# A transformer layer with dense experts on eight cores: layernorm's square root, squares and applies moved from ScalarE to VectorE, and one rope moved to GpSimd

## The chip, the cores and the metric

The kernel runs on all 8 cores of one Trainium2 chip. Each core takes one of the 8 batch rows (4096 tokens of 1024 channels) and runs the same program; the cores do not talk to each other. The metric is the device time of the slowest core in microseconds. The weights are loaded by every core from f32 in HBM and kept in bf16.

## What is computed

Per batch row, with `ln` a layernorm over the 1024 channels (eps 1e-5):

```python
h = ln(x)
q, k, v = h @ Wq, h @ Wk, h @ Wv               # 16 heads of 64
q, k = rope(silu(q)), rope(silu(k))
energy = einsum('bnhd,bmhd->bhnm', q, k) * tril
o = einsum('bhnm,bmhd->bnhd', energy, v)
o = o * sigmoid(h @ Wg1 @ Wg2)
x = x + ln((ln(o) * gamma + beta) @ Wo)
t = ln(x)
w = softmax over the top 2 of 8 of silu(t @ rw1 + rb1) @ rw2 + rb2
y = t + sum_e w_e * (silu(t @ ew1[e] + eb1[e]) @ ew2[e] + eb2[e])
x = x + ln(y)
```

The energy has no softmax, so the kernel computes attention chunk by chunk with a running state of k times v. There are five layernorms for every token.

## The kernel before

The program has three stages, each a block of its own. An `emit` records an instruction for one engine, with the tokens (semaphore and count) that it waits for; the five queues run in the order of recording. VectorE, ScalarE and GpSimd instructions always wait for the instruction before them on their own engine, through the engine's own semaphore, in addition to what `after` names.

**Attention (stage A)** works through 32 chunks of 128 tokens. For each i it records the front of chunk i and then the back of chunk i-1.

- `emit_front`: the tables cos and sin come by DMA (SP's queue, after both ropes of the chunk before). `emit_ln_stats` makes rstd and -mean*rstd of x (VectorE sum, ScalarE Square with accumulator, four small VectorE steps L298 to L307, Sqrt on ScalarE L310, reciprocal and two products on VectorE L313 to L318). ScalarE applies them (L378), PE transposes, ScalarE copies, PE does the q, k and v projections (L399, L410, L429), ScalarE applies Silu to q and k (L417, L421) and Tanh to the gate (L459). VectorE copies v (L463) and does q's rope (six instructions, L333 to L343), GpSimd does k's rope with the same helper, VectorE finishes the gate (L475). PE transposes q and k (L481, L490). Then 16 heads follow one another: energy on PE (L506), mask on VectorE (L513), three matmuls on PE. At the end VectorE updates the state (L537, L542) and makes `og`, output times gate (L545).
- `emit_back`: layernorm of `og` (apply L565), transposes (L573), the product with Wo (L583) into the PSUM tile pbig0, its layernorm (apply L600), the sum x1 with the residual (L604) and its store and the load of a later x on SP, layernorm of x1 (apply L619), a store of t, transposes (L629) and a copy into `tT`, which stays in SBUF for all 4096 tokens.

The four layernorms of a chunk use one scratch tile of columns for the front and one for the back. On VectorE the back of chunk i-1 is recorded behind the whole front of chunk i, so its first step runs after L545 of chunk i.

**Router (stage B)** computes the expert weights; the diff does not touch it.

**Experts (stage C)** goes over two groups of 2048 tokens. Each group first puts the weighted bias into `yac` for 16 chunks (PE L873, ScalarE copy L889), then all 8 experts run for all tokens (PE L909 and L946, Silu on ScalarE L920, the weighted sum on VectorE L959). Then comes the tail: for each of 16 chunks SP loads x1 and t (L977, L980) once the store of the chunk before has landed, VectorE adds t (L983), `emit_ln3` makes the statistics (Square L828 on ScalarE, sum L831 and small steps L833 to L842 on VectorE, Sqrt L845, then L848 to L853), ScalarE applies (L994), VectorE adds x1 (L997), SP stores.

Of the kernel before, what the change touches and what calls it, by code (L numbers as in the profile page):

```python
# [127 lines left out]
def build(debug=False, n_chunks=NCH, phases="ABC", stage=999):  # L128
# [32 lines left out]
    with ExitStack() as octx:  # L161
# [9 lines left out]
        with ExitStack() as actx:  # L171
# [118 lines left out]
            def emit_ln_stats(colbuf, src_ap, after_tok, psum_src=False):  # L290
                c_sx, c_sq, c_m, c_a, c_msq, c_b, c_s, c_rs, c_mrs, c_nmrs = range(10)
# [6 lines left out]
                t_m = s.emit(V, lambda e: e.tensor_scalar(  # L298
                    colbuf[:, c_m:c_m + 1], colbuf[:, c_sx:c_sx + 1], 1.0 / E, None,
                    ALU.mult), after=[t_sx])  # L300
                t_a = s.emit(V, lambda e: e.tensor_scalar(
                    colbuf[:, c_a:c_a + 1], colbuf[:, c_sq:c_sq + 1], 1.0 / E, EPS,
                    ALU.mult, ALU.add), after=[t_sq])
# [751 lines left out]
```

How the kernel before makes its waits and increments, by code:

```python
            def body(eng):  # L90
                waited = {}
                for waits, fn, semname, inc in recs[ename]:
                    for s, v in waits:
                        if waited.get(s, 0) >= v:
                            continue
                        eng.wait_ge(sems[s], v)
                        waited[s] = v
                    inst = fn(eng)
                    inst.then_inc(sems[semname], inc)
                for s, v in extra_final:
                    if waited.get(s, 0) >= v:
                        continue
                    eng.wait_ge(sems[s], v)
                    waited[s] = v
```

## Time and profile before

| | us |
|---|---|
| median of 6 runs | 7287.3 (7280.26 to 8089.09) |
| profiled execution, its own time | 7279.65 |
| its span, slowest core | 7277.9 |
| spans of the eight cores | 7258.9 to 7277.9 |
| busy in that span: PE, DVE, ACT, POOL | 4893.5, 1390.4, 1572.2, 299.0 |

PE is TensorE, DVE VectorE, ACT ScalarE, POOL GpSimd, SP the sync engine whose queue issues most DMAs. The times include a few microseconds around the span. Busy shares are averages over stages with different limits, so the stages are read one by one: attention lasts until 2828 us, the router until 3121 us, the experts of the first group until 4966.7 us, its tail until 5198.6 us; the second group's tail begins after 7042 us.

### The profile page before, as it was taken

How to read it: one execution, taken by the hardware profiler on the slowest of the kernel's cores; microseconds unless marked ns; L12 is line 12 of the kernel's file. 1: busy time of each engine (PE TensorE's matmuls, PEld its weight loads, DVE VectorE, ACT ScalarE, POOL GpSimd, SP SyncE). 2: the span in 40 equal slices, each digit the busy share in tenths (PEclk: the TensorE clock that was granted, in tenths of full speed). 3: DMA queues.
4: the chain of work that ended last, by engine and by line, in shares of the span. 5: the costliest groups of instructions: out<-in, count | busy, mean ns of one | idle time of the engine just before them, and what ended most of it. 6: DMA issues, size and time to landing. Idle time of an engine off the chain costs nothing.

```text
span 7277.9 us, 62772 instructions; the slowest of 8 cores (7258.9 to 7277.9 us)
## 1 busy us (share of the span) xinstructions
PE 4893.5 (67%) x22618; PEld 2257.1 (31%) x23024; DVE 1390.4 (19%) x2892; ACT 1572.2 (22%) x2185; POOL 299.0 (4%) x236
## 2 busy tenths in 40 slices
PE   3444344444444445479999999992399999999960
PEld 1222222222222222224444444441144444444430
DVE  1232322322323221210000000002100000000013
ACT  1222222222222222222211121111212211122111
POOL 1000001100000000000000000000000000000000
PEclk7666666666666666689999999996699999999985
DMA  3000000000000001022202222011111222112202
GB/s 60 21 21 21 27 25 21 21 21 21 21 21 25 26 21 21 1 51 47 47 10 38 47 47 47 16 31 58 58 24 24 47 47 47 25 23 47 47 22 90
DMA packets 92129, 241.52 MB, mean 33 GB/s; under 512 B 7528, under 2 KB 7784, under 8 KB 91824
## 3 DMA queue, kind: packets, MB, share of 16 engines
q0 software_dynamic: 54096, 136.65, 10.8%
q1 hardware_dynamic: 37728, 100.83, 4.1%
q8 instruction: 189, 3.10, 0.2%
q14 instruction: 116, 0.95, 0.0%
HBM read 332.15 MB, written 41.94 MB: 51 GB/s over the span
## 4 chain that ended last, share of the span: by engine, by line
PE 49%; DMA 3%; DVE 2%; ACT 2%; issue 1%; SPq 0%; DVEq 0%; ACTq 0%; POOLq 0%
PE peo L946 24%; PE peh L909 24%; DMA tc<-ts 2%; DMA out<-x1c 1%; ACT ehb L920 1%; ACT ylnb L994 1%; DVE yf L983 1%; DVE sc L831 1%; DVE x1c L997 1%; PE peo L873 0%; ACT yac L889 0%; SPq L977 0%; DVEq L96 0%; ACT sc L845 0%; DVE sc L848 0%
## 5 line engine op out<-in xcount | busy, mean ns | idle before, releaser
L946 PE MATMUL peo<-ew_bf,ehb 128*128 128x512 bf16 x8028 | 1769.4, 379 | 76.7 <-ACT ehb L920 68.2
L909 PE MATMUL peh<-tT,ew_bf 128*128 128x512 bf16 x8028 | 1772.4, 379 | 9.4 <-issue 0.7
L920 ACT ACTIVATE ehb<-peh,eb_sb 128x512 bf16<-128x512 f32 x1024 | 704.2, 688 | 2851.8 <-PE peh L909 2851.7
L946 PEld LDWEIGHTS peo<-ew_bf,ehb 128*128 128x128 bf16 x8192 | 797.1, 98 | 1049.0 <-issue 97.5
L909 PEld LDWEIGHTS peh<-tT,ew_bf 128*128 128x128 bf16 x8192 | 802.0, 98 | 970.9 <-issue 6.8
L959 DVE SCALAR_TENSOR_TENSOR yac<-peo,wsb,yac 128x1024 bf16<-128x1024 f32 x256 | 328.7, 1284 | 3368.6 <-PE peo L946 3356.6
L518 PE MATMUL pbig<-vb,eT 128*128 128x64 bf16 x512 | 108.8, 213 | 279.1 <-DVE eT L513 279.1
L629 PE MATMUL ptr<-identbf,sb_o 128*128 128x128 bf16 x256 | 32.4, 306 | 391.2 <-ACT sb_o L619 391.2
L513 DVE TENSOR_TENSOR eT<-pm,trium 128x128 bf16<-128x128 f32 x512 | 149.4, 292 | 638.6 <-PE pm L506 638.6
L573 PE MATMUL ptr<-identbf,sb_o 128*128 128x128 bf16 x256 | 32.4, 306 | 286.4 <-ACT sb_o L565 286.4
L873 PE MATMUL peo<-eb_bf,wTsb 8*128 8x512 bf16 x64 | 31.8, 595 | 277.1 <-ACT yac L889 269.8
L310 ACT ACT_TABLE_LOAD x32 | 41.1, 1283 | 812.6 <-DVE scol L307 812.6
L399 PE MATMUL pbig<-Wq_bf,ln1T 128*128 128x512 bf16 x511 | 171.5, 509 | 40.3 <-ACT ln1T L390 40.3
L583 PE MATMUL pbig<-Wo_bf,qT 128*128 128x512 bf16 x480 | 161.9, 496 | 51.7 <-ACT qT L576 51.7
L481 PE MATMUL ptr<-identbf,qro 128*128 128x128 bf16 x256 | 32.4, 306 | 239.2 <-DVE qro L343 239.2
L506 PE MATMUL pm<-qT,kTt 64*128 64x128 bf16 x512 | 144.7, 283 | 39.9 <-ACT kTt L493 39.9
L518 PEld LDWEIGHTS pbig<-vb,eT 128*128 128x128 bf16 x512 | 53.4, 104 | 359.7 <-issue 359.7
L385 PE MATMUL ptr<-identbf,ln1b 128*128 128x128 bf16 x256 | 32.4, 306 | 193.2 <-ACT ln1b L378 193.2
L629 PEld LDWEIGHTS ptr<-identbf,sb_o 128*128 128x128 bf16 x256 | 24.8, 138 | 399.8 <-issue 399.8
L808 POOL DMA_DIRECT2D ew_bf<-ew x15 | 13.2, 878 | 3278.7 <-PE peh L909 3278.7
L695 PE MATMUL pr<-tT,rw_bf 128*128 128x512 bf16 x498 | 132.1, 430 | 21.2 <-DMA rw_bf<-rw 19.4
L333 POOL TENSOR_TENSOR kt<-ks,sinb 128x512 f32<-128x512 f32 x32 | 40.4, 1262 | 2448.2 <-PE pbig L429 2357.8
(138 smaller groups left out, 3180.0 us busy)
## 6 DMA issues: line engine op xcount, KB each, us to landing
ew_bf<-ew POOLq DMA_DIRECT2D x30, 4096.0 KB, 26.3
xb<-x SPq DMA_DIRECT2D x32, 512.0 KB, 4.2
x1s<-x1b SPq DMA_DIRECT2D x32, 512.0 KB, 2.9
x1c<-x1s SPq DMA_DIRECT2D x32, 512.0 KB, 3.8
out<-x1c SPq DMA_DIRECT2D x32, 512.0 KB, 2.6
cosb<-cosr SPq DMA_DIRECT2D x32, 256.0 KB, 2.8
sinb<-sinr SPq DMA_DIRECT2D x32, 256.0 KB, 3.0
ts<-sb_o SPq DMA_DIRECT2D x32, 256.0 KB, 2.0
```

Source lines behind the costliest of these rows:

```text
L399: return e.matmul(pbig0[:, nh * 512:(nh + 1) * 512], ln1T[:, k, :], Wq_bf[:, k, nh * 512:(nh + 1) * 512], start=(k == 0), stop=(k == KT - 1))
L506: e.matmul(pe_slot[:, 128:256], kTt[po:po + 64, tile, :], qT[po:po + 64, tile, :], start=True, stop=True),
L513: e.tensor_tensor(eT[:, slot, :], pe_slot[:, 128:256], trium[:, :], ALU.mult),
L518: t_intra_last = s.emit(T, lambda e, h=h, slot=slot: e.matmul(pbig1[:, h * 64:(h + 1) * 64], eT[:, slot, :], vb[:, h * 64:(h + 1) * 64], s ...
L583: return e.matmul(pbig0[:, nh * 512:(nh + 1) * 512], qT[:, k, :], Wo_bf[:, k, nh * 512:(nh + 1) * 512], start=(k == 0), stop=False)
L695: return e.matmul(pr[:, :], rw1_bf[:, k, m * 128:(m + 1) * 128], tT[:, k, t8 * 512:(t8 + 1) * 512], start=(k == 0), stop=(k == KT - 1))
L831: t_sx = s3.emit(V, lambda e: e.reduce_sum(sc3[:, c_sx:c_sx + 1], src_ap, axis=AX.X), after=after_tok)
L909: return e.matmul(ph[:, :], ew1_bf[:, k, m * 128:(m + 1) * 128], tT[:, k, tstart:tstart + 512], start=(k == 0), stop=(k == KT - 1))
L920: e.activation(ehb[:, m, :], ph[:, :], AF.Silu, bias=eb1_sb[:, eidx, m:m + 1]),
L946: return e.matmul(po[:, nh * 512:(nh + 1) * 512], ehb[:, k, sub * 128:(sub + 1) * 128], ew2_bf[:, k, nh * 512:(nh + 1) * 512], start=(k == ...
L959: return e.scalar_tensor_tensor(yac[:, ci, :], po[:, :], wsb[:, ch0 + ci, eidx:eidx + 1], yac[:, ci, :], ALU.mult, ALU.add)
L983: t_y = s3.emit(V, lambda e, ci=ci: e.tensor_tensor(yf[:, :], yac[:, ci, :], tc[:, :], ALU.add), after=[t_tc, t_yacc_last[ci]] + ([t_prev_ ...
```

## The change

Three edits, in stage A and in the tail of stage C.

- Sqrt on ScalarE and reciprocal on VectorE are replaced by a reciprocal square root made of VectorE instructions on one column: a first guess from the bits of the number (five instructions) and three Newton steps of four instructions. This holds for all five layernorms.
- The apply moves from ScalarE (scale and bias) to VectorE (subtract the mean, multiply by rstd) for all layernorms but the front one, which keeps ScalarE and the two products (`emit_nmrs`). The squares of the og and x1 layernorms move to VectorE; those of x, of Wo's output and of the tail stay on ScalarE. In the tail the sum is now recorded before the Square.
- q's rope moves from VectorE to GpSimd, where it is recorded ahead of k's.

```diff
+            def emit_rsqrt(colbuf, c_v, c_out, after):
+                ci = colbuf[:, :].bitcast(I32)
+                t = s.emit(V, lambda e: e.tensor_scalar(
+                    ci[:, 20:21], ci[:, c_v:c_v + 1], 1, None,
+                    ALU.logical_shift_right), after=after)
+                s.emit(V, lambda e: e.tensor_copy(colbuf[:, 21:22], ci[:, 20:21]))
+                s.emit(V, lambda e: e.tensor_scalar(
+                    colbuf[:, 22:23], colbuf[:, 21:22], -1.0, MAGIC,
+                    ALU.mult, ALU.add))
+                s.emit(V, lambda e: e.tensor_copy(ci[:, 23:24], colbuf[:, 22:23]))
+                s.emit(V, lambda e: e.tensor_copy(
+                    colbuf[:, c_out:c_out + 1], ci[:, 23:24].bitcast(F32)[:, 0:1]))
+                for _ in range(3):
+                    s.emit(V, lambda e: e.tensor_tensor(
+                        colbuf[:, 20:21], colbuf[:, c_out:c_out + 1],
+                        colbuf[:, c_out:c_out + 1], ALU.mult))
+                    s.emit(V, lambda e: e.tensor_tensor(
+                        colbuf[:, 21:22], colbuf[:, c_v:c_v + 1],
+                        colbuf[:, 20:21], ALU.mult))
+                    s.emit(V, lambda e: e.tensor_scalar(
+                        colbuf[:, 22:23], colbuf[:, 21:22], -0.5, 1.5,
+                        ALU.mult, ALU.add))
+                    t = s.emit(V, lambda e: e.tensor_tensor(
+                        colbuf[:, c_out:c_out + 1], colbuf[:, c_out:c_out + 1],
+                        colbuf[:, 22:23], ALU.mult))
+                return t
...
-                t_sq = s.emit(S, lambda e: e.activation(
-                    dump[:, :], src_ap, AF.Square,
-                    accum_out=colbuf[:, c_sq:c_sq + 1]),
-                    after=after_tok + ([t_sx] if psum_src else []))
+                if sq_eng == "S":
+                    t_sq = s.emit(S, lambda e: e.activation(
+                        dump[:, :], src_ap, AF.Square,
+                        accum_out=colbuf[:, c_sq:c_sq + 1]),
+                        after=after_tok + ([t_sx] if psum_src else []))
+                else:
+                    t_sq = s.emit(V, lambda e: e.scalar_tensor_tensor(
+                        dump[:, :], src_ap, 1.0, src_ap, ALU.mult, ALU.mult,
+                        accum_out=colbuf[:, c_sq:c_sq + 1]), after=after_tok)
...
-                t_s = s.emit(S, lambda e: e.activation(
-                    colbuf[:, c_s:c_s + 1], colbuf[:, c_b:c_b + 1], AF.Sqrt),
-                    after=[t_b])
-                t_rs = s.emit(V, lambda e: e.reciprocal(
-                    colbuf[:, c_rs:c_rs + 1], colbuf[:, c_s:c_s + 1]), after=[t_s])
...
+                t_rs = emit_rsqrt(colbuf, c_b, c_rs, [t_b])
+                return ([t_rs], colbuf[:, c_rs:c_rs + 1],
+                        colbuf[:, c_m:c_m + 1])
...
+                ln_toks, rs_ap, nmrs_ap = emit_nmrs(scol, ln_toks)
...
-                t_ropeq = emit_rope(V, qs, rt2, qro,
+                t_ropeq = emit_rope(GP, qs, rt2, qro,
...
-                t_oln = s.emit(S, lambda e, rs_ap=rs_ap, nmrs_ap=nmrs_ap,
-                               ogs=ogs:
-                               e.activation(sb_o[:, :], ogs, AF.Identity,
-                                            bias=nmrs_ap, scale=rs_ap),
+                    sq_eng="V")
+                t_oln = s.emit(V, lambda e, rs_ap=rs_ap, m_ap=m_ap, ogs=ogs:
+                               e.tensor_scalar(sb_o[:, :], ogs, m_ap, rs_ap,
+                                               ALU.subtract, ALU.mult),
```

The applies `t_aoln`, `t_tb` and, in the tail, `t_yln` change in the same way as `t_oln`; the x1 layernorm has `sq_eng="V"` too; `emit_ln3` gets its own copy of the reciprocal square root.

## Rows read from the trace of the kernel before

In the view of stretches (rows 1) the columns are the stretch and its length, the busy us of each engine with its instructions in brackets, PEclk, the DMA share and GB/s. In a timeline (rows 2, 3, 4, 6) they are start and busy us, engine, line, operation, tiles, count, and in brackets the idle time before with what ended it. In the view of groups (rows 5) busy us and mean ns of one stand behind the first bar, idle us before them behind the second.

**Rows 1.** Busy time by stretch: attention, experts of group 0, both tails.
```profile
70.00:2828.00 2758.00, 1175.50 (x5704) 586.59 (x5768) 838.11 (x1928) 681.91 (x867) 260.46 (x192) 0.62 0.06 21
3121.00:4966.70 1845.70, 1781.56 (x8060) 801.62 (x8224) 163.06 (x127) 369.60 (x529) 14.14 (x14) 0.99 0.21 37
4966.70:5198.60 231.90, 0.67 (x3) 0.11 (x2) 76.50 (x160) 42.82 (x66) 0.00 (x0) 0.51 0.24 85
7042.00:7277.90 235.90, 0.00 (x0) 0.00 (x0) 77.54 (x161) 42.80 (x65) 0.00 (x0) 0.51 0.24 86
```

**Rows 2.** Timeline, one chunk, the layernorm of og (L310 is its Sqrt).
```profile
1568.74 1.22 DVE L292 TENSOR_REDUCE scol<-og 128x1 f32<-128x1024 f32 x1
...
1571.15 1.28 ACT L310 ACT_TABLE_LOAD   x1 [25.35 <-DVE scol L307]
...
1572.45 0.20 ACT L310 ACTIVATE scol<-scol 128x1 f32<-128x1 f32 x1
...
1574.98 1.01 PE L573 MATMUL ptr<-identbf,sb_o 128*128 128x128 bf16 x8 [9.00 <-ACT sb_o L565]
```

**Rows 3.** Timeline, the same chunk: attention-output, x1 and front layernorms.
```profile
1585.84 0.15 DVE L301 TENSOR_SCALAR scol<-scol 128x1 f32<-128x1 f32 x1 [1.05 <-ACT dump L294]
...
1586.36 0.16 DVE L307 TENSOR_TENSOR scol<-scol 128x1 f32<-128x1 f32 x1
...
1589.08 1.23 DVE L604 TENSOR_TENSOR x1b<-sb_o,xb 128x1024 f32<-128x1024 bf16 x1 [1.47 <-ACT sb_o L600]
...
1590.40 1.22 DVE L292 TENSOR_REDUCE scol<-x1b 128x1 f32<-128x1024 f32 x1
...
1595.31 1.01 PE L629 MATMUL ptr<-identbf,sb_o 128*128 128x128 bf16 x8 [12.12 <-ACT sb_o L619]
...
1599.35 0.16 DVE L307 TENSOR_TENSOR scol<-scol 128x1 f32<-128x1 f32 x1
...
1600.69 1.24 ACT L378 ACTIVATE ln1b<-xb,scol 128x1024 bf16<-128x1024 f32 x1 [0.89 <-DVE scol L318]
```

**Rows 4.** Timeline, the front of the chunk before: Silu, ropes, first energy matmul.
```profile
1524.23 1.28 ACT L417 ACT_TABLE_LOAD   x1 [5.71 <-PE pbig L399]
...
1527.76 1.02 ACT L421 ACTIVATE ks<-pbig 128x1024 f32<-128x1024 f32 x1 [1.21 <-PE pbig L410]
...
1529.05 1.26 POOL L333 TENSOR_TENSOR kt<-ks,sinb 128x512 f32<-128x512 f32 x1 [77.05 <-PE pbig L429]
...
1533.16 1.51 POOL L339 TENSOR_TENSOR kt<-ks,cosb 128x512 f32<-128x512 f32 x1
...
1542.45 1.01 PE L490 MATMUL ptr<-identbf,kro 128*128 128x128 bf16 x8 [1.25 <-ACT qT L485]
...
1544.71 0.26 PE L506 MATMUL pm<-qT,kTt 64*128 64x128 bf16 x1 [1.25 <-ACT kTt L493]
```

**Rows 5.** Groups of instructions by line and shape, VectorE and GpSimd.
```profile
L542 DVE CAST Sbf<-Sf 128x512 bf16<-128x512 f32 x32 | 13.7, 428 | 3.3
...
L262 DVE TENSOR_SCALAR Wo_bf<-Wo_bf,gamma_sb 128x1024 bf16<-128x1024 bf16 x8 | 3.9, 486 | 67.9 <-ACT bWo_row L257 67.2
...
L736 DVE SCALAR_TENSOR_TENSOR tpw<-tpw,l_sb 128x8 f32<-128x8 f32 x32 | 5.3, 167 | 3.7 <-DVE tpw L733 0.5
...
L748 DVE TENSOR_TENSOR tpw<-tpw 128x8 f32<-128x8 f32 x32 | 5.3, 167 | 6.3 <-DVE tpw L742 5.7 <-ACT tpw L745 0.6
...
L339 POOL TENSOR_TENSOR kt<-ks,cosb 128x512 f32<-128x512 f32 x32 | 48.6, 1518 | 4.6
```

**Rows 6.** Timeline, tail of group 0: one chunk, and its last.
```profile
5017.60 0.16 DVE L842 TENSOR_TENSOR sc<-sc 128x1 f32<-128x1 f32 x1
...
5020.36 1.23 DVE L997 TENSOR_TENSOR x1c<-ylnb,x1c 128x1024 f32<-128x1024 bf16 x1 [1.51 <-ACT ylnb L994]
...
5193.66 1.06 ACT L828 ACTIVATE tc<-yf 128x1024 bf16<-128x1024 f32 x1 [9.75 <-DVE yf L983]
...
5198.58 1.01 ACT L889 CAST yac<-peo 128x1024 bf16<-128x1024 f32 x1
```

More of the change, by code:

```diff
@@ L10 @@
 BF16 = mybir.dt.bfloat16
+I32 = mybir.dt.int32
 AF = mybir.ActivationFunctionType
@@ L288, in build @@
             }
[L290 to L291 removed]
+            MAGIC = float(0x5F3759DF)
+            def emit_rsqrt(colbuf, c_v, c_out, after):
[24 more added lines that the diff above has]
+                return t
@@ L304, in emit_ln_stats @@
+                    EPS, ALU.mult, ALU.add), after=[t_sq])
                 t_msq = s.emit(V, lambda e: e.tensor_tensor(
@@ L824, in build, with emit_rsqrt3 @@
             t_out_final = []
+            MAGIC3 = float(0x5F3759DF)
+            def emit_rsqrt3(colbuf, c_v, c_out, after):
+                ci = colbuf[:, :].bitcast(I32)
+                t = s3.emit(V, lambda e: e.tensor_scalar(
+                    ci[:, 10:11], ci[:, c_v:c_v + 1], 1, None,
+                    ALU.logical_shift_right), after=after)
+                s3.emit(V, lambda e: e.tensor_copy(colbuf[:, 11:12], ci[:, 10:11]))
+                s3.emit(V, lambda e: e.tensor_scalar(
+                    colbuf[:, 12:13], colbuf[:, 11:12], -1.0, MAGIC3,
+                    ALU.mult, ALU.add))
+                s3.emit(V, lambda e: e.tensor_copy(ci[:, 13:14], colbuf[:, 12:13]))
+                s3.emit(V, lambda e: e.tensor_copy(
+                    colbuf[:, c_out:c_out + 1], ci[:, 13:14].bitcast(F32)[:, 0:1]))
+                for _ in range(3):
+                    s3.emit(V, lambda e: e.tensor_tensor(
+                        colbuf[:, 10:11], colbuf[:, c_out:c_out + 1],
+                        colbuf[:, c_out:c_out + 1], ALU.mult))
+                    s3.emit(V, lambda e: e.tensor_tensor(
+                        colbuf[:, 11:12], colbuf[:, c_v:c_v + 1],
+                        colbuf[:, 10:11], ALU.mult))
+                    s3.emit(V, lambda e: e.tensor_scalar(
+                        colbuf[:, 12:13], colbuf[:, 11:12], -0.5, 1.5,
+                        ALU.mult, ALU.add))
+                    t = s3.emit(V, lambda e: e.tensor_tensor(
+                        colbuf[:, c_out:c_out + 1], colbuf[:, c_out:c_out + 1],
+                        colbuf[:, 12:13], ALU.mult))
+                return t
             def emit_ln3(src_ap, after_tok):
-                c_sx, c_sq, c_m, c_a, c_msq, c_b, c_s, c_rs, c_mrs, c_nmrs = range(10)
+                c_sx, c_sq, c_m, c_a, c_msq, c_b, c_rs = 0, 1, 2, 3, 4, 5, 6
+                t_sx = s3.emit(V, lambda e: e.reduce_sum(
+                    sc3[:, c_sx:c_sx + 1], src_ap, axis=AX.X), after=after_tok)
                 t_sq = s3.emit(S, lambda e: e.activation(
@@ L844, in emit_ln3 @@
                     sc3[:, c_msq:c_msq + 1], ALU.subtract), after=[t_a, t_msq])
-                t_s = s3.emit(S, lambda e: e.activation(
-                    sc3[:, c_s:c_s + 1], sc3[:, c_b:c_b + 1], AF.Sqrt),
-                    after=[t_b])
-                t_rs = s3.emit(V, lambda e: e.reciprocal(
-                    sc3[:, c_rs:c_rs + 1], sc3[:, c_s:c_s + 1]), after=[t_s])
-                t_mrs = s3.emit(V, lambda e: e.tensor_tensor(
-                    sc3[:, c_mrs:c_mrs + 1], sc3[:, c_m:c_m + 1],
-                    sc3[:, c_rs:c_rs + 1], ALU.mult), after=[t_rs])
-                t_nmrs = s3.emit(V, lambda e: e.tensor_scalar(
-                    sc3[:, c_nmrs:c_nmrs + 1], sc3[:, c_mrs:c_mrs + 1], -1.0,
-                    None, ALU.mult), after=[t_mrs])
-                return ([t_rs, t_nmrs], sc3[:, c_rs:c_rs + 1],
-                        sc3[:, c_nmrs:c_nmrs + 1])
+                t_rs = emit_rsqrt3(sc3, c_b, c_rs, [t_b])
+                return ([t_rs], sc3[:, c_rs:c_rs + 1], sc3[:, c_m:c_m + 1])
             slot_guard = [None] * CPG
```

66 lines of the change are left out of this document (36 added, 30 removed).

## The prediction

> **What bounds the kernel now.** I read the stretches first, to see which engine is full where. The reader is to see two kinds of stage [rows 1]: in the expert stage TensorE is busy for 1781.6 of 1845.7 us, so nothing that VectorE or ScalarE does there counts; in the attention stage (2758 us for 32 chunks) the busiest engine has 1175 us, and in the two tails (231.9 and 235.9 us for 16 chunks each) no engine has more than 79. Those stages are one chain of waits, and every microsecond added to a link is paid 32 times. So I went on to the timeline of one chunk (the period is 85.7 us) and of one tail chunk, and followed what starts what. Five layernorms per token chunk lie on that chain: four in attention, one in the tail. None is covered: after each of them PE or the next VectorE step starts within 0.2 us.
>
> **Part 1: the square root goes from ScalarE to 17 VectorE instructions.** What goes is Sqrt and reciprocal, and, where the apply moves to VectorE, also the two that make the negated product of mean and rstd. Before, from the start of L307 (the variance) to the next large step it takes 1.34 us in the front layernorm (1599.35 to 1600.69), 2.72 us for the attention-output one including its apply (1586.36 to 1589.08) [rows 3], and 2.76 us in the tail with its apply (5017.60 to 5020.36) [rows 6].
> What comes is 5 instructions for the first guess and 3 x 4 for Newton's steps, all on 128x1, each reading what the last wrote, so each waits on VectorE's own semaphore as the old ones do. Such instructions stand 0.26 us apart: two steps, L301 to L307, take 0.52 [rows 3]. Twelve of the 17 are of the slightly longer kind (0.16 us as L307, against 0.15 as L301), so I take 0.265: 17 x 0.265 = 4.50 us. The casts between int32 and f32 and the shift on 128x1 are not in the trace; the bounds are the 0.25 and 0.27 us of neighbours, a difference of 0.3 us a layernorm either way.
>
> **Part 2: the apply on VectorE.** From SBUF (f32 in, bf16 out): a cast of that kind on 128x512 takes 428 ns [rows 5], which at two elements a 0.96 GHz cycle is 267 + 161. So 1024 elements take 533 + 161 = 0.69 us. Scalars read per partition cost more: L262 takes 486 ns for 1024 bf16, where a quarter of 1024 cycles is 267 and the same 161 leaves 58 for one of them [rows 5]. With two, 0.06 to 0.12; I take 0.10: 0.79 us. From PSUM at one element a cycle (the reduce of equal size takes 1.22): 1.33 us. ScalarE took 1.20 to 1.24 and two hops between engines.
>
> **Part 3: the square on VectorE** (the og and x1 layernorms). It lay beside VectorE's reduce and now stands behind it. The trace has scalar_tensor_tensor on two f32 inputs in SBUF only at 128x8 (L736), 167 ns, no more than a tensor_tensor of that shape (L748) [rows 5], where two cycles an element would show as 8 ns. So I take one, 1.23 us as in the full-width f32 step L604 [rows 3], + 0.10 to the next start, and the read of the accumulator, which the trace shows only for ScalarE; bounds nothing and 0.2, I take 0.10: 1.43. The upper bound for the whole is two cycles an element, 1.07 more.
>
> **Each layernorm from these pieces** (reduce 1.22 + 0.10; the four small steps 1.05; gap to PE 0.15):
> - og: before 6.24 us from reduce to PE (1568.74 to 1574.98) with a table load of 1.28 in it [rows 2]. After 1.32 + 1.43 + 1.05 + 4.50 + 0.79 + 0.15 = 9.24: **+3.00**.
> - attention output, square still on ScalarE: 0.26 + 4.50 + 1.33 + 0.10 = 6.19 against 2.72: **+3.47**.
> - x1: 9.24 against 4.91 (1590.40 to 1595.31) [rows 3]: **+4.33**.
> - front: apply stays on ScalarE with both extra products; Sqrt and reciprocal took 0.57 of the 1.34 (the two products, 0.27 + 0.26, the variance 0.25): 4.50 - 0.57 = **+3.93**. Its reduce waits behind the longer x1 chain on VectorE, but its Square, behind the copy into tT on ScalarE, is later still, so nothing more is lost; the x load (issued after x1) has had 10 us by then.
> - tail: 0.26 + 4.50 + 0.79 + 0.10 = 5.65 against 2.76: **+2.89**. Reduce now stands before Square in program order, but on two engines; no effect.
>
> **The table loads.** og's Sqrt no longer displaces Silu's table: the 1.28 us in front of it were on the chain and their removal is in the 6.24 above. The load before Silu at 1524.23 goes as well; V's matmuls had to wait for K's anyway, so it gives nothing there, but the q rope can start earlier. The Trainium skill, page ScalarE: Activation LUTs, section What ACT_TABLE_LOAD costs, puts a set switch at 1283 ns plus a drain, some 2.66 us in all; by it og would gain 1.4 us more a chunk (an estimate: 44 us over the kernel). The timeline disagrees: the load starts at 1571.15 and is done in 1.28, and L310's Sqrt starts at 1572.45, at once; the sum keeps 1.28.
>
> **Part 4: q rope on GpSimd, ahead of k rope.** What is queued behind it on GpSimd is k rope, and k's transposes wait for that, then the copy, then the first energy matmul at 1544.71. Before, both ropes ran beside each other. VectorE and GpSimd took turns: GpSimd's first instruction takes 1.26 us, the same shape beside VectorE's f32 work 1.52 [rows 4, 5]. Alone, three of them need 4.11 (1529.05 to 1533.16), two ropes 4 x 4.11 - 0.14 = 16.3. Start: Silu of q at 1524.23, 1.02 long, plus 0.27 as between L421's end (1528.78) and GpSimd: 1525.5. End 1541.8, plus 0.25 for the gate's conversion that comes between: 1542.1. k's transposes to energy take 2.26 (1542.45 to 1544.71), plus 0.1: 1544.4 against 1544.71, **-0.3 us**. Bounds: -0.6 without the gate; +2.6 if all twelve run at the 1.52 pace (19.4 us for the two ropes). I take -0.3, since the short instructions ran while VectorE was idle or reading PSUM, and that is what it does now. VectorE, free of the rope, does only V's copy and the gate there and then waits for energy, so its 7 us are no gain. The mask steps (16 of them, one chain with PE) don't change. SP's table loads wait on both ropes of the chunk before and have 15 us to spare. TensorE's granted clock, 0.62 over the attention stage and 0.51 in the tails [rows 1], is low there because it idles; its matmuls start after idle stretches before and after, and I count nothing.
>
> **Sum.** Attention: 3.00 + 3.47 + 4.33 + 3.93 - 0.3 = 14.43 x 32 = +462. Tails: 31 x 2.89 = +89.6; the last chunk of group 0 costs nothing, since ScalarE is free after its Square (5193.66 + 1.16 = 5194.8) instead of at 5198.58, and group 1's bias copies follow [rows 6]: -3.7; two Sqrt loads less, -2.6. Together +83. Total +545 us. The profiled execution took 7279.65 us (span 7277.9), so 7825; the median of the runs is 7.6 higher, so I forecast **7833 us**, 7.5% slower.
>
> **Rivals.**
> - *Square at half rate.* 1.07 us more in two layernorms x 32 = +68: **7901 us**. The 128x8 row speaks against it, but it has no accumulator. The Trainium skill, page Vector Engine (DVE) Microarchitecture Reference, section Points that are easy to get wrong, says that scalar_tensor_tensor with two non-bf16 SBUF sources halves throughput, for want of a port for the accumulator; no run here shows it yet. Chance 0.13.
> - *Ropes at the contended pace.* 2.9 more than forecast x 32 = +93: **7926 us**. For it: half of the six are at 1.4 to 1.52 in every chunk. Against: they are those with VectorE's instruction between them. Chance 0.06.
> - *Cheaper than summed.* The accumulator read and the second scalar cost nothing and the rope gains 0.6: (2 x 0.1 + 3 x 0.05 + 0.3) x 32 = -21, and small instructions at 0.25: 17 x 5 x 32 x 0.015 = -41: **7771 us**. Chance 0.10.
> - *Faster than before.* Small steps would have to overlap: there are 17 x 5 x 32 = 2720 of them, so the sum turns at 0.265 - 545/2720 = 0.065 us each, below the 0.15 that one is busy. With each at 0.05 us the time would be 7833 - 2720 x 0.215 = **7248 us**. Chance 0.01.
> - *The table loads stay*, because Silu and Tanh turn out to need separate sets: no row of before has a load between them, and at one exposed load a chunk, 32 x 1.28 = +41: **7874 us**. Chance 0.02.
>
> The forecast keeps 0.68, with its own range of 7795 to 7870. The range over the cases leaves out only the contended ropes, the overlap and the edge of the others: 7765 to 7915. What a measurement of this kernel tells from no change is about 0.2%, 15 us; all likely cases are far above: faster 0.01, same 0.01, slower 0.98.
>
> **What would show it.** In the profile after: 17 instructions of 128x1 at 0.26 to 0.27 apart between variance and apply; VectorE's apply at 0.75 to 0.85 us (1.3 from PSUM); the square near 1.25 and not 2.3; no table load in attention after the first; GpSimd's twelve rope instructions at 1.16 to 1.26; the energy matmul 20.2 us after the q matmuls end; a chunk period near 100.1 us; a tail chunk 2.9 longer; expert stage unchanged. Wrong would be: a square of over 2 us, GpSimd at 1.5, or a period below 95, which would mean that part of a layernorm was covered after all.

## The result and the profile after

The changed kernel takes **7864.3 us** (median of 5, lowest 7861.5): 1.0798 times the kernel before, with a 95% interval of 1.0781 to 1.0815. I had forecast 7833 and 7765 to 7915. Executions in which some cores ran at a lower clock than the others are left out of every comparison, and where an experiment has only such a profile, its cores of undisturbed clock are compared with the same cores of before. The profiled execution took 7865.01 us, its span on core 5 7863.4 (7277.9 before, so +585.5).

The head of the page gives the busy us of each engine. Between the slowest cores (4 before, 5 after) ScalarE lost 351 us and VectorE gained 349. TensorE's 4893.5 us of before lack the records of 406 matmuls; core 5 has all 23024 in both traces, and there TensorE, which was given nothing new to compute, went from 4915.5 to 4950.0 us, 34.5 more:

```profile
PE 4950.0 (63%) x23024; PEld 2256.7 (29%) x23024; DVE 1739.7 (22%) x5260; ACT 1221.1 (16%) x1702; POOL 514.5 (7%) x428
```

The view of stretches, for attention, the experts of group 0 and the two tails (columns as in [rows 1]):

```profile
91.00:3243.00 3152.00, 1187.90 (x5649) 575.42 (x5649) 1037.11 (x3625) 371.35 (x437) 476.00 (x384) 0.59 0.05 18
3627.80:5478.70 1850.90, 1792.86 (x8226) 801.71 (x8226) 164.34 (x128) 369.22 (x529) 14.11 (x14) 0.99 0.22 37
5478.70:5739.40 260.70, 0.00 (x0) 0.00 (x0) 117.06 (x376) 17.24 (x30) 0.00 (x0) 0.51 0.21 76
7586.60:7863.40 276.80, 0.00 (x0) 0.00 (x0) 124.53 (x401) 18.39 (x32) 0.00 (x0) 0.50 0.20 73
```

Cut at the same instructions in both traces (core 4 before, core 5 after, the slowest of each), the stages differ as follows:

| stage | before | after | difference | forecast |
|---|---|---|---|---|
| start to the first q matmul | 86.4 | 91.7 | +5.3 | (in the +462) |
| attention, up to the router | 2742.5 | 3244.6 | +502.1 | +462 |
| router | 293.1 | 291.6 | -1.5 | 0 |
| experts, both groups | 3657.1 | 3662.3 | +5.2 | 0 |
| tails with group 1's bias copies | 498.8 | 573.2 | +74.4 | +83 |

So the signs and the places are as forecast, attention is 45 us dearer than I said and the tails 9 cheaper. Now the timeline of one chunk. First the layernorm of og, to be laid beside [rows 2]:

```profile
1629.35 1.22 DVE L323 TENSOR_REDUCE scol<-og 128x1 f32<-128x1024 f32 x1
...
1630.68 1.23 DVE L331 SCALAR_TENSOR_TENSOR dump<-og 128x1024 bf16<-128x1024 f32 x1
...
1631.83 0.08 DVE L331 DVE_READ_ACCUMULATOR dump<-og 128x1 f32 x1
...
1632.02 0.15 DVE L334 TENSOR_SCALAR scol<-scol 128x1 f32<-128x1 f32 x1
...
1633.07 0.15 DVE L295 TENSOR_SCALAR scol<-scol 128x1 int32<-128x1 int32 x1
...
1637.26 0.16 DVE L315 TENSOR_TENSOR scol<-scol 128x1 f32<-128x1 f32 x1
...
1637.59 0.81 DVE L604 TENSOR_SCALAR sb_o<-og,scol 128x1024 bf16<-128x1024 f32 x1 [0.18 <-DVE scol L315]
...
1638.55 1.01 PE L612 MATMUL ptr<-identbf,sb_o 128*128 128x128 bf16 x8 [11.96 <-DVE sb_o L604]
```

The 17 instructions of the reciprocal square root stand between L295 and the apply: the first 16 steps from 1633.07 to 1637.26 are 0.262 each, and with the last one the apply starts 4.52 us after the first. Nothing else is in that time; each is 0.15 or 0.16 us of work and 0.1 of waiting for the one before. From reduce to PE the layernorm takes 9.20 us.

The same timeline further on: variance and apply of Wo's output, then x1, then the front (beside [rows 3]):

```profile
1650.22 0.16 DVE L343 TENSOR_TENSOR scol<-scol 128x1 f32<-128x1 f32 x1
...
1654.94 1.34 DVE L639 TENSOR_SCALAR sb_o<-pbig,scol 128x1024 bf16<-128x1024 f32 x1
...
1656.46 1.23 DVE L644 TENSOR_TENSOR x1b<-sb_o,xb 128x1024 f32<-128x1024 bf16 x1 [0.17 <-DVE sb_o L639]
...
1657.79 1.22 DVE L323 TENSOR_REDUCE scol<-x1b 128x1 f32<-128x1024 f32 x1
...
1667.12 1.01 PE L670 MATMUL ptr<-identbf,sb_o 128*128 128x128 bf16 x8 [20.07 <-DVE sb_o L659]
...
1671.15 0.16 DVE L343 TENSOR_TENSOR scol<-scol 128x1 f32<-128x1 f32 x1
...
1676.39 1.24 ACT L417 ACTIVATE ln1b<-xb,scol 128x1024 bf16<-128x1024 f32 x1 [5.86 <-DVE scol L356]
```

And the front behind it, q matmuls, Silu, ropes and the first energy (beside [rows 4]):

```profile
1680.03 6.40 PE L438 MATMUL pbig<-Wq_bf,ln1T 128*128 128x512 bf16 x16 [1.25 <-ACT ln1T L429]
...
1686.59 1.02 ACT L456 ACTIVATE qs<-pbig 128x1024 f32<-128x1024 f32 x1 [6.70 <-PE pbig L438]
...
1687.81 1.26 POOL L371 TENSOR_TENSOR rt<-qs,sinb 128x512 f32<-128x512 f32 x1 [85.35 <-PE pbig L449]
...
1696.21 1.54 POOL L371 TENSOR_TENSOR kt<-ks,sinb 128x512 f32<-128x512 f32 x1 [0.33 <-ACT th L498]
...
1703.38 1.15 POOL L381 TENSOR_TENSOR kro<-kro,kt 128x512 bf16<-128x512 bf16 x1
...
1704.79 1.01 PE L529 MATMUL ptr<-identbf,kro 128*128 128x128 bf16 x8 [8.15 <-POOL kro L381]
...
1707.05 0.26 PE L545 MATMUL pm<-qT,kTt 64*128 64x128 bf16 x1 [1.25 <-ACT kTt L532]
```

The wait of 6.70 us in front of L456, the Silu, ends with the q matmuls, and no table load stands there any more. From its start to the first energy matmul it takes 20.46 us, against 20.48 from load to energy in [rows 4]. The tail, one chunk (beside [rows 6]):

```profile
7590.30 0.16 DVE L912 TENSOR_TENSOR sc<-sc 128x1 f32<-128x1 f32 x1
...
7595.02 0.81 DVE L1053 TENSOR_SCALAR ylnb<-yf,sc 128x1024 bf16<-128x1024 f32 x1
...
7596.01 1.23 DVE L1057 TENSOR_TENSOR x1c<-ylnb,x1c 128x1024 f32<-128x1024 bf16 x1 [0.17 <-DVE ylnb L1053]
```

Link by link, in the chunk shown, in us:

| link | before | after | measured | forecast |
|---|---|---|---|---|
| og layernorm | 6.24 | 9.20 | +2.96 | +3.00 |
| attention output | 2.72 | 6.24 | +3.52 | +3.47 |
| x1 layernorm | 4.91 | 9.33 | +4.42 | +4.33 |
| front | 1.34 | 5.24 | +3.90 | +3.93 |
| Silu to energy | 20.48 | 20.46 | -0.02 | -0.30 |
| tail, a chunk of 16 | 2.76 | 5.71 | +2.95 | +2.89 |

The five of attention sum to 14.78 x 32 = 473 us (forecast 462). One chunk is a sample: in this one x1's 4.42 has a stray 0.19 us between two of its small steps. Summed over all 32 chunks and averaged over the eight cores, the four layernorms grew by 96.6 (og), 114.8, 135.7 (x1) and 126.3 us (front), that is 3.02, 3.59, 4.24 and 3.95 a chunk; with the rest of the path that is 473.5 us, so the sum holds.

The stage grew by 507 with its start. The 34 us between are in no link of my list. They are in the matmuls themselves, which the groups show, first before and then after, core 5 in both (matmuls, busy us, mean ns of one, idle before). Before:

```profile
L399 PE MATMUL pbig<-Wq_bf,ln1T 128*128 128x512 bf16 x512 | 168.5, 502 | 39.9 <-ACT ln1T L390 39.9
...
L583 PE MATMUL pbig<-Wo_bf,qT 128*128 128x512 bf16 x512 | 171.9, 497 | 39.9 <-ACT qT L576 39.9
```

After:

```profile
L438 PE MATMUL pbig<-Wq_bf,ln1T 128*128 128x512 bf16 x512 | 194.4, 563 | 39.9 <-ACT ln1T L429 39.9
...
L622 PE MATMUL pbig<-Wo_bf,qT 128*128 128x512 bf16 x512 | 180.1, 515 | 39.9 <-ACT qT L615 39.9
```

One such matmul lasts 379 ns at TensorE's upper clock level (2.4 GHz) and 631 at the lower (1.2 GHz), and they start 216 or 427 ns apart, so a rise of 1 ns in the mean costs 0.84 ns of path. The mean rose by 61 ns for q and 18 for Wo: 79 x 0.84 x 16 matmuls x 32 chunks = 34 us. That these 34 and the 473 make the 507 of the table exactly is partly luck, since the table compares two cores. The timelines give the same without it: from its first weight load to its last matmul the q projection, and from its first weight load to the reduce behind it the Wo projection, got longer by 23.2 and 10.8 us over the 32 chunks in the mean of the eight cores, together 34.0 (30 on core 0, 39 on core 5), where attention up to its last transposes grew by 507.5 (502 and 515).

Two stretches, the q matmuls of one chunk, before and then after, show it as a granted clock (last but two), 0.67 (core 4) against 0.56 (core 5), where 0.5 is 1.2 GHz and 1.0 is 2.4. Before:

```profile
1604.30:1609.70 5.40, 5.32 (x16) 2.10 (x18) 0.00 (x0) 0.00 (x0) 0.00 (x0) 0.67 0.00 0
```

After:

```profile
1680.00:1686.50 6.50, 6.47 (x18) 2.42 (x19) 0.00 (x0) 0.00 (x0) 0.00 (x0) 0.56 0.00 0
```

TensorE stood idle, but for its transposes, for 21 us ahead of the first (1583.2 to 1604.3) and for 33 us ahead of the second (1647.1 to 1680.0). But the clock is not a plain function of that time even within one kernel: on core 5 the q projection took 4.94 to 6.08 us from chunk to chunk before, always behind 21.3 to 22.1 us, and 4.94 to 6.60 after, always behind 33.1 to 33.8 (chunks 3 to 32).

### The profile page after: what moved, and what is told of

It is laid out like the page before. It is cut to its first block, busy times and chain, and to the rows that moved or that the text cites. A ratio compares the mean times of both kernels' runs of the same rounds, so it can differ in the third digit from the quotient of the medians.

```text
span 7863.4 us, 66662 instructions; the slowest of 8 cores (7841.8 to 7863.4 us)
## 1 busy us (share of the span) xinstructions
PE 4950.0 (63%) x23024; PEld 2256.7 (29%) x23024; DVE 1739.7 (22%) x5260; ACT 1221.1 (16%) x1702; POOL 514.5 (7%) x428
## 4 chain that ended last, share of the span: by engine, by line
PE 41%; DMA 7%; DVE 3%; issue 1%; ACT 1%; DVEq 0%; SPq 0%; ACTq 0%; POOLq 0%
PE peo L1005 23%; PE peh L968 18%; DMA ew_bf<-ew 4%; DMA tc<-ts 1%; DMA out<-x1c 1%; DVE yf L1042 1%; DVE x1c L1057 0%; DVE sc L898 0%; ACT ehb L979 0%; PE peo L932 0%; ACT yac L948 0%; DVE ylnb L1053 0%; DVEq L97 0%; DVE sc L885 0%; DVE sc L891 0%
## 5 line engine op out<-in xcount | busy, mean ns | idle before, releaser
L612 PE MATMUL ptr<-identbf,sb_o 128*128 128x128 bf16 x256 | 32.4, 307 | 382.5 <-DVE sb_o L604 382.5
L438 PE MATMUL pbig<-Wq_bf,ln1T 128*128 128x512 bf16 x512 | 194.4, 563 | 39.9 <-ACT ln1T L429 39.9
L371 POOL TENSOR_TENSOR rt<-qs,sinb 128x512 f32<-128x512 f32 x32 | 40.4, 1262 | 2690.0 <-PE pbig L449 2599.0
L622 PE MATMUL pbig<-Wo_bf,qT 128*128 128x512 bf16 x512 | 180.1, 515 | 39.9 <-ACT qT L615 39.9
L615 ACT COPY qT<-ptr 128x1024 bf16<-128x1024 bf16 x32 | 32.4, 1012 | 1082.0 <-PE ptr L612 1082.0
L529 PE MATMUL ptr<-identbf,kro 128*128 128x128 bf16 x256 | 32.4, 305 | 254.1 <-POOL kro L381 254.1
L545 PE MATMUL pm<-qT,kTt 64*128 64x128 bf16 x512 | 144.7, 283 | 39.9 <-ACT kTt L532 39.9
L502 DVE CAST vb<-pbig 128x1024 bf16<-128x1024 f32 x32 | 39.2, 1225 | 538.5 <-PE pbig L468 538.5
```

The costliest lines, as they stand in the source:

```text
L371: s.emit(eng, lambda e: e.tensor_tensor(s2[:, :, :], x2v, sin_v, ALU.mult), after=after_toks)
L438: return e.matmul(pbig0[:, nh * 512:(nh + 1) * 512], ln1T[:, k, :], Wq_bf[:, k, nh * 512:(nh + 1) * 512], start=(k == 0), stop=(k == KT - 1))
L545: e.matmul(pe_slot[:, 128:256], kTt[po:po + 64, tile, :], qT[po:po + 64, tile, :], start=True, stop=True),
L622: return e.matmul(pbig0[:, nh * 512:(nh + 1) * 512], qT[:, k, :], Wo_bf[:, k, nh * 512:(nh + 1) * 512], start=(k == 0), stop=False)
```

## The experiments

The theory after the result: the path grew by chains of small dependent instructions, the ropes are neutral, and the 34 us are time at the lower clock, which I put down to the longer idle stretches. The rivals: the square or the apply costs more than its row shows, the rope costs something that is given back elsewhere, or the 34 us are something else in attention. In all of them "A" is the attention stage on core 0, where it took 2739.8 us before and 3237.4 after (+497.6), and q/Wo are the means of one matmul on core 0, 506/501 ns before and 556/513 after. On core 0 the clock term is (50 + 12) x 0.84 x 512 = 27 us by these means and 30 by the timelines. In the traces of the experiments the first Wo matmul of each chunk is not recorded on core 0 (480 of 512, as the idle time before the group, 52.0 for 39.9, shows too); it took 585 ns on average in the two kernels, so the Wo means of the experiments are some 2 to 6 ns too low. Where it matters, the lengths of the projections in the timeline are given beside them.

**e1, fewer Newton steps.** One step instead of three; the output is less exact.

```diff
-                for _ in range(3):
+                for _ in range(1):
```

> The changed kernel with one Newton step instead of three in every reciprocal square root (two of the three steps are left out, so the output is less exact). Chain theory: eight instructions of 128x1 at 0.263 us are gone from four layernorms of each of 32 chunks and from 31 of the tails' 32: 8 x 0.263 x 159 = 335 us less, and with the shorter idle stretches the q projection a little shorter too (TensorE's clock theory: up to 15 us more): 7515 to 7530 us. Rival (part of the chain was covered by other work): clearly less than 335 us less, above 7600 us.

Measured 7511.0 and 7518.3 us, 346 to 353 less than the changed kernel; A 2958.0, q/Wo 542/513. Eight instructions fewer in five layernorms are 8 x 0.262 x 160 = 335 us; q's mean fell by 14 ns, which is 6 us. In the timelines the og, attention-output and x1 layernorms each got 68 to 69 us shorter over 32 chunks, 0.27 us an instruction. The price per instruction holds.

**e2, the squares back on ScalarE.** The rest as changed.

```diff
-                    sq_eng="V")
+                    sq_eng="S")
```

> The changed kernel with the squares of the og and x1 layernorms back on ScalarE. Chain theory: the step from the square to the small ones falls from 1.34 to 0.07 us, twice a chunk: 64 x 1.27 = 81 us less, about 7783 us. Rival (the square on VectorE was hidden behind something else): within 15 us of 7864.

Measured 7779.1 to 7787.8, ratio to before 1.0693 (1.0674 to 1.0712), A 3157.1. The two squares cost 80 us of the change, some 1.25 us each, one pass with its start and not two. The rival of half rate is out.

**e3, q's rope back on VectorE.** The rest as changed.

```diff
-                t_ropeq = emit_rope(GP, qs, rt2, qro,
+                t_ropeq = emit_rope(V, qs, rt2, qro,
```

> The changed kernel with q's rope back on VectorE. Chain theory: both routes reach the first energy matmul about 20.5 us after the q projection, so no change: 7855 to 7875 us. Rival (two ropes in a row on GpSimd are what makes the chunk longer than summed): about 40 us less, 7825 us. Rival on the other side (the table load removed before Silu had made the move pay): 40 us more, 7905 us.

Measured 7864.0 and 7864.4, A 3237.2 against 3237.4. The move of the rope is worth nothing in either direction.

**e4, Sqrt and reciprocal back.** Both in all five layernorms; squares, applies and rope as changed.

```diff
-                t_rs = emit_rsqrt(colbuf, c_b, c_rs, [t_b])
+                t_s = s.emit(S, lambda e: e.activation(
+                    colbuf[:, 9:10], colbuf[:, c_b:c_b + 1], AF.Sqrt),
+                    after=[t_b])
+                t_rs = s.emit(V, lambda e: e.reciprocal(
+                    colbuf[:, c_rs:c_rs + 1], colbuf[:, 9:10]), after=[t_s])
```

> The changed kernel with Sqrt on ScalarE and reciprocal on VectorE in place of the 17 instructions, everything else as changed. Chain theory: 159 layernorms each 3.9 us shorter (-620), table loads back: 1.28 us a chunk in front of Sqrt on og's path (+41) and 1.28 us a chunk in front of Silu, now on the path because q's rope on GpSimd starts from it (+41), tails +3, and the 40 us that the colder q and Wo projections cost given back: 7290 us, as the kernel before within 40 us. Rival (apply and square on VectorE carry most of the loss): above 7500 us.

Measured 7365.8 in one execution, and cores 0 to 3 of the profiled one at 7316.9 to 7332.1 (7258.9 to 7275.6 before): Sqrt gives back about 500 of the change's 585 us, but this is 40 to 75 above what I expected. A is 2829.6, +89.8 to before, and q/Wo are 552/556. I had thought that the clock loss would go with the 17 instructions. It is larger here, 101 ns x 0.84 x 512 = 43 us by the means and 49 by the timeline. Most of the rest is the 35 us by which the way from the q matmuls to the first energy matmul is longer: the table load stands in front of Silu again, now on the path (e7). The layernorms themselves end up near where they were (og +9, attention output -12, x1 +9 us over 32 chunks). In this chunk (timeline) the second eight of Wo's matmuls take 2.59 us, where they took 1.90 before (1580.97) and after the change (1644.83), all at the upper level:

```profile
1541.18 2.59 PE L626 MATMUL pbig<-Wo_bf,qT 128*128 128x512 bf16 x8
```

That speaks against my account of the clock: TensorE's idle time ahead of og's transposes is 294.8 us over the 32 chunks here and 382.5 in the changed kernel, where Wo's mean was 513.

**e7, the rope alone.** The kernel before with only q's rope on GpSimd.

```diff
-                t_ropeq = emit_rope(V, qs, rt2, qro,
+                t_ropeq = emit_rope(GP, qs, rt2, qro,
```

> The kernel before with only q's rope moved to GpSimd. Chain theory: the rope now starts from q's Silu, and in front of that still stands a table load of 1.28 us; the first energy matmul comes 1.28 us later than in either kernel: 32 x 1.28 = +41, about 7326 us. Rival (moving the rope is neutral by itself): 7285 us. Rival (it frees VectorE and gains): below 7270 us.

Measured 7344 to 7367, ratio 1.0111 (1.0086 to 1.0137); A 2802.9, +63.1. The timeline says why the same edit costs nothing in the changed kernel and 1% here:

```profile
1556.29 1.28 ACT L417 ACT_TABLE_LOAD   x1 [6.15 <-PE pbig L399]
...
1557.58 1.02 ACT L417 ACTIVATE qs<-pbig 128x1024 f32<-128x1024 f32 x1
...
1558.81 1.26 POOL L333 TENSOR_TENSOR rt<-qs,sinb 128x512 f32<-128x512 f32 x1 [71.56 <-PE pbig L410]
...
1577.78 0.26 PE L506 MATMUL pm<-qT,kTt 64*128 64x128 bf16 x1 [1.25 <-ACT kTt L493]
```

The load precedes Silu of q, which both ropes on GpSimd now wait for: from load to energy 21.49 us instead of 20.48 in the chunks shown, 1.01 x 32 = 32; over all chunks of core 0 the way from the q matmuls to the energy grew by 36. While k's rope started GpSimd's work, the load lay under the k matmuls. The matmuls got slower too:

```profile
L399 PE MATMUL pbig<-Wq_bf,ln1T 128*128 128x512 bf16 x511 | 181.1, 532 | 40.3 <-ACT ln1T L390 40.3
...
L583 PE MATMUL pbig<-Wo_bf,qT 128*128 128x512 bf16 x480 | 175.2, 528 | 52.0 <-ACT qT L576 52.0
```

53 ns x 0.84 x 512 = 23 us. That would leave 8 of the 63 open, but both readings are too low: in the timeline the two projections grew by 27.7 us (Wo's mean lacks its first matmuls, which ran at the lower level), and 36 + 28 = 64 is the whole. And this rise comes with no longer idle stretch at all. The group of og's transposes on core 0 (behind the second bar the idle time), in the kernel before:

```profile
L573 PE MATMUL ptr<-identbf,sb_o 128*128 128x128 bf16 x256 | 32.4, 306 | 286.2 <-ACT sb_o L565 286.2
```

and in e7:

```profile
L573 PE MATMUL ptr<-identbf,sb_o 128*128 128x128 bf16 x256 | 32.4, 306 | 285.4 <-ACT sb_o L565 285.4
```

It is the same within 1 us over 32 chunks, and so is that ahead of the transposes of x1 (391.1 and 390.5) and of the front (193.1 and 193.2), and q/Wo went from 506/501 to 532/528. The part of my theory that names the longer idle stretches as the cause of the clock loss falls, at least as the only cause; that the loss is one of the clock still had to be tested.

**e5 and e6, keeping TensorE busy ahead of the front's transposes.** 44 (e5, in the changed kernel) or 24 (e6, in the one before) matmuls of 256 columns whose result nobody reads, from the second chunk on.

```diff
+                if c > 0:
+                    for _ in range(44):
+                        s.emit(T, lambda e: e.matmul(
+                            pm7[:, 256:512], identbf[:, :],
+                            Wq_bf[:, 0, 0:256], start=True, stop=True))
                 t_tr = None
                 for j in range(KT):
```

> The changed kernel plus 44 matmuls of 128x256 whose result nobody reads, on TensorE in its idle stretch before the transposes of the front layernorm (from chunk 1 on). Clock theory: the q projection, 6.1 to 6.4 us now, starts at the high clock and takes 3.6: 31 x 2.6 = 80 us less, about 7784 us; together with the twin run on the kernel before, the distance of the two kernels falls from 585 to about 555 us. Rival (the 40 us beyond the sum come from something else on the path): q projection unchanged or the distance stays at 585.

> The kernel before plus 24 such matmuls at the same place. Clock theory: the q projection falls from 5.4 to 3.6 us: 31 x 1.8 = 56 us less, about 7228 us. Rival: unchanged, 7285 us.

Both missed. e5 took 7840.6 to 7863.7, ratio 1.079 (1.0764 to 1.0816), with q/Wo 534/501; e6 took 7259 to 7297, ratio 0.999 (0.9958 to 1.0021), with 511/494. In e5 the 44 matmuls ended 3.43 us before the transposes began, and q took 6.07 us in the chunk that I looked at (core 2); over the chunks of core 0 the pause was 2.6 to 4.3 us and q took 4.95 to 6.59. In e6 they ended later, timeline of core 2:

```profile
1672.68 5.14 PE L385 MATMUL pm<-Wq_bf,identbf 128*128 128x256 bf16 x24
1678.64 0.61 PE L390 MATMUL ptr<-identbf,ln1b 128*128 128x128 bf16 x8 [0.82 <-ACT ln1b L378]
1680.50 5.30 PE L404 MATMUL pbig<-Wq_bf,ln1T 128*128 128x512 bf16 x16 [1.25 <-ACT ln1T L395]
```

In e6 the transposes take 0.61 us and not 1.01, so they ran at 2.4 GHz, and yet q's 16 matmuls take 5.30, as long as with no filling. Between the transposes and q lie the 1.25 us of ScalarE's copy. The clock had been up; it stayed up through that pause and for the first 0.4 us of q's matmuls, and then fell, though TensorE was busy again. The view of stretches (granted clock last but two):

```profile
1680.50:1680.90 0.40, 0.40 (x2) 0.19 (x3) 0.00 (x0) 0.00 (x0) 0.00 (x0) 1.00 0.00 0
1680.90:1681.30 0.40, 0.40 (x2) 0.14 (x1) 0.00 (x0) 0.00 (x0) 0.00 (x0) 0.52 0.00 0
```

So neither run held the clock where it was meant to, and they say nothing yet on the 34 us.

**e9 and e10, the pause filled too.** 31 and 10 such matmuls ahead of and behind the transposes in the kernel before (e9), 74 and 10 in the changed one (e10).

```diff
+                if c > 0:
+                    for _ in range(10):
+                        s.emit(T, lambda e: e.matmul(
+                            pm7[:, 256:512], identbf[:, :],
+                            Wq_bf[:, 0, 0:256], start=True, stop=True))
```

> The kernel before plus 31 matmuls of 128x256 without a reader before the front layernorm's transposes and 10 behind them, during the copy into ln1T, so that TensorE works without a gap until the q projection. Clock theory: the q projection starts at 2.4 GHz and takes 3.6 us instead of 5.3 to 5.5: 31 x 1.8 = 56 us less and the transposes 0.4 us each less (12): 7205 us. Rival (the clock drops whatever TensorE does, as it did in the run with a pause): as that run, 7259 us.

> The changed kernel with 74 and 10 such matmuls at the same places. Clock theory: the q projection takes 3.6 us instead of 6.1 to 6.4: 31 x 2.6 = 80 us less, transposes 12 less: 7772 us; the distance to the held version of the kernel before falls from 585 to about 565 us. Rival: 7840 us, distance as before.

Measured 7221.0 and 7223.4 (e9) and 7784.6 (e10). The timeline of e10 (core 6) shows no idle time ahead of the transposes or during the copy (the first q matmul, in the 0.37 us, is not recorded), and 15 q matmuls in 3.40 us:

```profile
1723.39 10.27 PE L424 MATMUL pm<-Wq_bf,identbf 128*128 128x256 bf16 x74
1733.52 0.61 PE L429 MATMUL ptr<-identbf,ln1b 128*128 128x128 bf16 x8
1733.96 1.25 PE L436 MATMUL pm<-Wq_bf,identbf 128*128 128x256 bf16 x10
1735.59 3.40 PE L448 MATMUL pbig<-Wq_bf,ln1T 128*128 128x512 bf16 x15 [0.37 <-ACT ln1T L439]
```

The groups, core 0, of e9:

```profile
L409 PE MATMUL pbig<-Wq_bf,ln1T 128*128 128x512 bf16 x481 | 111.5, 385 | 12.6 <-ACT ln1T L400 12.4 <-issue 0.2
```

and of e10:

```profile
L448 PE MATMUL pbig<-Wq_bf,ln1T 128*128 128x512 bf16 x481 | 110.5, 383 | 12.8 <-ACT ln1T L439 12.8
```

Both q projections now run at 2.4 GHz throughout. The distance between changed kernel and kernel before is then 7783.1 - 7221.5 = 561.6 us by spans, not 585.5: 24 less. On core 0 q's share of the clock term was 50 x 0.84 x 512 = 22.

Whole spans also hold the stages behind attention, which scatter by some 8 us from core to core, and e10 has a single execution. Attention alone, in the mean of the eight cores, is the closer test: there the difference fell from 507.5 to 474.6 us, and 474.6 is what the links gave without any clock (473.5). Both projections together differ by -4.5 us now, where it was +34.0. For q that was the purpose. For Wo it is chance: nothing was put ahead of it, its length in the changed kernel stayed (-1 us), and in e9 it grew by 12 to 16 us over the kernel before (q fell by 49 to 55), with the same idle time ahead (286.1 and 286.2). So the clock term is shown for what it is, and that an edit at one projection moves the clock of the other shows again that the idle time ahead doesn't fix it.

**e8, e11, e12, the applies of the change with the rest of before.** All three keep the applies on VectorE, and have Sqrt with reciprocal, the squares on ScalarE and the rope on VectorE. The Sqrt table is loaded by an unused Sqrt on a spare column, at the heads, where ScalarE has nothing to do:

```diff
                 prev["ptr_free"] = t_kT
+                s.emit(S, lambda e: e.activation(
+                    scol[:, 30:31], identbf[:, 0:1], AF.Sqrt))
```

e11 is this alone. e8 adds 24 unread matmuls ahead of the front's and of og's transposes; e12 has 35 ahead and 10 behind at the front, 44 and 10 at og, without a pause.

> A version meant to beat both: Sqrt and reciprocal as before, all squares on ScalarE, q's rope on VectorE, the applies on VectorE as changed (not the front one), a Sqrt on a spare column during the heads so that the table load is off og's path, and 24 matmuls without a reader before the transposes of the front and of the og layernorm. Chain theory against the kernel before: og -2.3, attention output -0.4, x1 -0.95 us a chunk (-116), tail -0.95 each and its last chunk (-33), q projection -1.8 and Wo projection -1.6 a chunk (-109): about 7029 us. Rival (the clock can't be held so, only the layernorms gain): 7135 us.

> The layernorm part of the version meant to beat both, without any extra matmul: Sqrt and reciprocal, squares on ScalarE, ropes as before, three applies and the tail's on VectorE, Sqrt on a spare column during the heads. Chain theory against the kernel before: -116 in attention, -33 in the tails, the shorter idle stretches leave the projections where they are or a little warmer: 7125 to 7140 us. Rival (the fast projections of the earlier version carried its gain): above 7200 us.

> That layernorm part plus 35 and 10 matmuls around the front transposes and 44 and 10 around og's, without a gap until each projection. Clock theory: q projection 3.6 us and Wo projection 3.8 instead of 5.2 and 5.6: 31 x 1.6 + 32 x 1.8 = 107 us below the version without them, about 7025 us. Rival (an added pause or a delay by the extra matmuls eats it): 7110 us as the earlier version.

| | us | ratio to before | A | q/Wo ns |
|---|---|---|---|---|
| e11 | 7158 to 7168 | 0.9851 (0.9822 to 0.988) | 2655.8 | 543/520 |
| e8 | 7113 to 7123 | 0.9782 (0.976 to 0.9804) | 2614.4 | 486/519 |
| e12 | 7149.8, lowest of six | none | | 383/379 (core 5) |

e11 and e8 are faster than both kernels. Both came out above their expectations, e11 by 20 to 30 us over the top of its range and e8 by some 90. The layernorms did as forecast: in e11 the three of attention got 113 us shorter on core 0 (forecast 116). What missed was the clock: e11's projections are slower than those before (56 ns x 0.84 x 512 = 24 us, 28 by the timeline), though the idle time ahead of og's transposes fell from 286.2 to 217.2 us and ahead of the front's stayed (193.1 and 193.5). e8 has the pause of e6, and its two projections together are longer than before (-8 and +12 us on core 0; the faster transposes give 22 back), where I had forecast -109. For e12, cores 4 to 7 of the profiled execution ran at 7000.5 to 7009.3 us, where the same cores took 7259.2 to 7277.9 before, 3.6% less. Against e11 these four cores are some 150 us faster in the mean (7004.8 against 7155.6), where I had expected 107: attention alone gives 148, of which the two projections give 137 and the two groups of transposes in front of them 25, and the unread matmuls take 15 back by delaying og's. A time of the whole kernel can't be given. The view of cores (span, mean granted clock), one core of each die:

```profile
core 0: 7140.8 us, clock 0.820
...
core 5: 7000.5 us, clock 0.838
```

and the groups of e12 on core 5, all matmuls of both projections at 2.4 GHz:

```profile
L646 PE MATMUL pbig<-Wo_bf,qT 128*128 128x512 bf16 x512 | 121.2, 379 | 5.0 <-ACT qT L639 5.0
...
L452 PE MATMUL pbig<-Wq_bf,ln1T 128*128 128x512 bf16 x512 | 117.6, 383 | 6.1 <-ACT ln1T L443 6.1
```

## Where the prediction held, and the step that failed

- **"Those stages are one chain of waits"** held. VectorE's 349 busy us more would be nothing for an engine that is a fifth busy; they and the waits between them came out nearly whole (473.5 us of links where I had 462). The expert stage, where TensorE is busy nearly all the time, moved by 5 us in both groups together.
- **Part 1, 17 x 0.265 = 4.50.** Measured 4.52, casts and shift between int32 and f32 included. At 17 x 0.262 x 160 they cost 713 us; e1 takes eight of the 17 out, which is 335 us by that price, and is 346 to 353 faster.
- **Part 2, the apply.** 0.81 us for 0.79, and 1.34 from PSUM for 1.33.
- **Part 3, the square.** 1.23 us and an accumulator read of 0.08; the next step starts 1.34 after the square (1630.68 to 1632.02), where I had 1.43. The rival of half rate would have given 7901 us; the row and e2 rule it out here. The Trainium skill, page Vector Engine (DVE) Microarchitecture Reference, section Points that are easy to get wrong, would halve the rate of this form; the trace doesn't agree, with 1.23 us for 1024 f32 elements read from SBUF, no more than the plain tensor_tensor of that width takes. Both sources are the same tile here; two different tiles were not run.
- **The table loads** went as forecast. The 1.28 us of og's load is in its 2.96; and e7 adds a thing I had not priced: the load before Silu was worth nothing only as long as Silu of k, behind the k matmuls, set GpSimd's start. In the changed kernel it is gone, which is what makes the rope's move free.
- **Part 4, "I take -0.3".** Measured -0.02, +9 us over the kernel: 0.26 us from GpSimd's last rope instruction to PE (1703.38 + 1.15 to 1704.79), where I had 0.1, and the gate's conversion slowed one GpSimd instruction from 1.26 to 1.54. e3 confirms the size: nothing.
- **"TensorE's granted clock [...] I count nothing."** This is the step that failed, a term left at zero that measured 34 us in the mean of the cores (30 on core 0, 39 on core 5), of the 40 by which the sum is short. I had seen that the matmuls start after idle stretches before and after, and concluded that nothing changes. But the q matmuls of before were not all at 1.2 GHz: the mean of 502 ns between 379 and 631 says that about half of them were at 2.4, and this share could fall. It fell to a quarter (563). e9 and e10, where it is all of them in both kernels, take 24 us out of the difference of the spans and 33 out of that of attention. The Trainium skill, page TensorE: Matmul & The Clock Gate, section What's actually happening, says that the clock follows how busy TensorE has been of late; the trace agrees as far as 21 us of idle time ahead of the q stretch gave 0.67 and 33 us gave 0.56. But the idle time doesn't order the runs: e7 has that of the kernel before and e11 less, and both have slower projections; and chunks of one kernel with the same idle time differ by over 1 us. So the size of the term, and that it is one of the clock, are shown; why it took this value in the changed kernel stays open, and I could not have computed it from the trace of before, only bounded it (core 0): with both projections at 379 ns (1007 - 758 = 249 less) -107 us, with both at 631 (255 more) +110.
- **The tails, +83.** Measured +74.4. The chain in them was a little dearer (2.95 against 2.89), but VectorE's wait for t's load got shorter: 219.0 us over 30 chunks before, 207.2 after. So 12 us were given back there, and I had counted none; that the transfers themselves were faster is not shown, the wait is what the trace shows.

Together: +34 clock, +9 rope, +2 from the four layernorms of attention, -9 in the tails, +4 in router and experts make up the 40 us between +545 and +585.5.

## What to carry to other kernels

In a stage that is one chain of waits, count the instructions on the chain and multiply by the spacing from start to start (0.26 us here), not by their work: 17 tiny instructions on one column cost nearly four passes over 1024 columns, and a table function on another engine with its load is cheaper, above all if the load is put into an idle stretch (e11, 1.5% faster). Look at the mean duration of matmuls that follow idle stretches: if it lies between the two clock levels, any edit that shifts the work around them can move it, and both levels belong in the range. An edit that was free beside another (the rope) may cost 1% alone.

## What was not expected of the hardware

- Unread matmuls ahead of the front's transposes brought nothing when the 1.25 us of the copy behind the transposes stayed idle (e6: 7259 to 7297 us, ratio 0.999, q at 511 ns), and 53 us of attention when there were 31, and 10 more in that pause (e9: A 2686.9 against 2739.8, q at 385). In e6 the granted clock stayed at 1.00 through the pause and fell 0.4 us into the matmuls behind it.
- With the time ahead of q filled, the other projection, Wo, got 12 to 16 us longer than in the kernel before (e9), though nothing had changed ahead of it.
- The projections got slower in every variant without filling, whether TensorE's idle stretches grew or shrank: 506/501 ns before, 532/528 in e7, 552/556 in e4, 543/520 in e11, 24 to 49 us by the timelines of core 0.
- VectorE's scalar_tensor_tensor with an accumulator on two f32 inputs from SBUF takes 1.23 us for 1024 elements, and its accumulator read 0.08, where ScalarE's read takes 0.19.
